# Routing weights of a tile computed beside its slot numbers instead of behind them

## The chip, the cores and the metric

The kernel runs on one core of a Trainium2 chip. The metric is the device time of one execution in microseconds (us), lower is better; the time of a kernel is the median of its runs. VectorE is DVE in the rows, ScalarE is ACT, TensorE is PE (its weight loads are PEld) and GpSimd is POOL.

## The reference, cut to what matters

The program is a block of four sublayers over 16 sequences of 112 tokens with 256 channels. The first is a transformer layer (self attention, cross attention to 375 context rows, gated feed-forward), the second a mixture of 64 experts with the best 8 for each token, the third a perceiver-like attention, the fourth a mixture of 8 experts with the best one. What the change touches is the router of the second sublayer:

```python
logits = jnp.einsum('bsh,he->bse', hidden_states, router_w)
affinity = jax.nn.sigmoid(logits)
top_scores, top_idx = jax.lax.top_k(affinity, K)                  # K = 8 of E = 64
top_w = top_scores / (jnp.sum(top_scores, axis=-1, keepdims=True) + 1e-09)
```

`top_w` is what the kernel calls `wgt`. It is used only in the third sublayer's stage, where the rows that the experts gave are added up (`add_rows`, L2034).

## The kernel before, in words

Each engine has a program of its own, and semaphores order them. Within an engine, instructions start in the order in which they are written. The first sublayer works on one sequence of 112 tokens ("batch" in the code) at a time: batch 0 is written out, batches 1 to 14 are a hardware loop, batch 15 is written out again. While batch b runs, the router works on the tile of batch b-1 (112 rows) in gaps that the code names by hand. The tile of batch 15 has no batch behind it: `tables0` does all its steps in a row.

The cross attention of a batch is the function `attention`. It has 16 heads, done as 8 pairs. Its loop has 9 steps on VectorE, s = 0 to 8. In step s PE writes the scores of pair s to PSUM (L759), VectorE takes their row maxima, two TENSOR_REDUCE to `nmax` (L1608), and ScalarE takes the exponentials (L1281). One step later PE transposes the probabilities (L774), VectorE and ScalarE copy one half each to `probsT` (L1612 and L1311), and one more step later PE multiplies them by the values (L786). ScalarE's order in a step is: exponential of the first head, copy of the pair before, exponential of the second head. PE's order in a step is: scores of pair s, transposes of pair s-1, outputs of pair s-2; the first three transposes wait for the two copies of the pair before and the first head's exponential, the next three for the second head's exponential.

At the end of step s VectorE calls `slots(r, 2s)` and `slots(r, 2s+1)` for the router's tile r. Calls 0 to 7 find the slot number of each of the 8 chosen experts, a SCALAR_TENSOR_TENSOR with an accumulator (L1697), call 0 also updates the counts (L1694), and call 8 casts the slot numbers to integers and releases them to GpSimd (L1701, `slots_ok`). GpSimd then copies them and issues 8 indirect DMAs that scatter the token numbers to a table in HBM (L536). Calls 8, 9, 10 and 12 also work out the weights: the sum of the 8 scores (L1703), plus 1e-9 (L1706), its reciprocal (L1709), and the product with the scores (L1712).

`settled()` waits until the last VectorE instruction that was issued through `note()` has finished writing, by a semaphore that VectorE raises itself; in the loop it takes a few register instructions to form the value waited for. Every slot call from 0 to 7 begins with one.

Behind the slot numbers of the last tile, `tables0` waits for the experts' counts, which PE forms once `slots_ok` is raised (L1004), and begins the block tables at L1810.

## Time and profile before

| what | value |
|---|---|
| median of 3 runs | 3499.01 us (3495.71 to 3500.59) |
| the profiled execution | 3510.26 us |
| its span, first to last instruction | 3508.5 us |
| mean granted TensorE clock | 0.926 of full speed |
| PE busy | 3049.2 us (87%) |
| DVE busy | 1495.2 us (43%) |
| ACT busy | 1078.9 us (31%) |
| POOL busy | 884.0 us (25%) |
| batches 1 to 15 in the trace | router step L1694 starts first at 179.5 us, then about every 98 us |

A row of a timeline has the start, the duration, the engine, the line, the operation, what it writes and reads, and how many instructions are merged in it; in square brackets stands how long the engine was idle before it, and what released it. "remote" there means that the profile shows no instruction whose end fits the release. A granted clock of 1.00 is TensorE at 2.4 GHz, 0.50 is 1.2 GHz.

### The profile page before, as it was taken

What the parts mean: (1) busy time and instruction counts of PE and PEld (TensorE: products, weight loads), DVE (VectorE), ACT (ScalarE), POOL (GpSimd) and SP (SyncE); (2) the same over time, 40 slices, a digit from 0 to 9 for tenths busy, and PEclk for the clock granted to TensorE, in tenths of its full rate; (3) what the DMA queues carried; (4) which work ended last, traced back from release to release, by engine and by line L of the source; (5) the groups of instructions that cost most, each with busy time, mean ns of one, the idle gap of its engine ahead of it and who ended that gap; (6) DMA issues with size and microseconds to landing.
All of it is one profiled execution on the core that took longest, in us unless ns stands there. A gap on an engine that the chain in (4) does not pass through costs nothing.

```text
span 3508.5 us, 59755 instructions
## 1 busy us (share of the span) xinstructions
PE 3049.2 (87%) x17314; PEld 2074.6 (59%) x17315; DVE 1495.2 (43%) x4297; ACT 1078.9 (31%) x2986; POOL 884.0 (25%) x1952
## 2 busy tenths in 40 slices
PE   6998989899898999885888885899999999995786
PEld 5666666666666666654666662555555555554564
DVE  3444444444444444444333332454544545434222
ACT  1333333333333333331222221343433434331111
POOL 0111111111111111112444443333242332401211
PEclk9999899999999999997999997899999999996898
DMA  5000000000000000003555541100000010002241
GB/s 191 5 3 6 4 6 6 6 6 6 6 1 6 4 6 6 6 2 102 162 171 172 152 104 37 30 15 30 15 24 21 15 30 15 15 1 84 99 149 56
DMA packets 89707, 155.44 MB, mean 44 GB/s; under 512 B 17072, under 2 KB 65072, under 8 KB 88112
## 3 DMA queue, kind: packets, MB, share of 16 engines
q1 hardware_dynamic: 39664, 85.56, 7.5%
q0 software_dynamic: 21184, 42.92, 4.8%
q10 hardware_dynamic: 28800, 26.23, 2.2%
q8 instruction: 32, 0.52, 0.1%
q14 instruction: 27, 0.22, 0.0%
HBM read 122.32 MB, written 32.32 MB: 44 GB/s over the span
## 4 chain that ended last, share of the span: by engine, by line
PE 74%; DVE 9%; issue 8%; ACT 3%; DMA 2%; another core or an unknown queue 2%; POOL 1%; DVEq 1%; POOLq 0%; SPq 0%; ACTq 0%
PE psG L812 12%; PE psG L806 11%; PE psG L800 11%; PE psG L822 7%; PE psG L1159 6%; PE psT L774 4%; PE psO L786 4%; PE psG L759 4%; DVE nmax L1608 3%; PE psO L1183 2%; PE psG L1165 2%; PE psO L1187 2%; ACT probs L1281 2%; PE psT L714 2%
## 5 line engine op out<-in xcount | busy, mean ns | idle before, releaser
L1281 ACT ACTIVATE probs<-psG,nmax 112x112 f32<-112x112 f32 (+2 forms) x768 | 403.8, 533 | 389.5 <-DVE nmax L1608 281.7
L812 PE MATMUL psG<-W,ctxT 128*125 128x512 f32 (+2 forms) x896 | 398.6, 593 | 0.0
L806 PE MATMUL psG<-ctxT,W 128*128 128x375 f32 (+1 forms) x1024 | 391.8, 530 | 1.1 <-ACT ctxT L1465 1.1
L800 PE MATMUL psG<-hT,W 128*128 128x112 f32 x2560 | 345.5, 293 | 45.9 <-issue 26.6
L1608 DVE TENSOR_REDUCE nmax<-psG 112x1 f32<-112x375 f32 (+1 forms) x512 | 287.2, 599 | 191.5 <-remote 106.1
L800 PEld LDWEIGHTS psG<-hT,W 128*128 128x128 f32 x2560 | 324.6, 206 | 71.8 <-issue 40.7
L774 PEld LDWEIGHTS psT<-ident,probs 112*125 112x125 f32 (+2 forms) x1792 | 215.5, 174 | 235.7 <-ACT probs L1281 133.6
L774 PE MATMUL psT<-ident,probs 112*125 112x112 f32 (+2 forms) x1792 | 275.4, 289 | 65.8 <-ACT probsT L1311 25.9
L806 PEld LDWEIGHTS psG<-ctxT,W 128*128 128x128 f32 x1024 | 189.8, 190 | 166.0 <-issue 114.6
L812 PEld LDWEIGHTS psG<-W,ctxT 128*125 128x125 f32 (+2 forms) x896 | 162.9, 186 | 187.7 <-issue 186.6
L759 PE MATMUL psG<-kT,qT 64*112 64x375 f32 (+1 forms) x1024 | 251.3, 568 | 11.5 <-ACT ctxT L1465 10.6
L786 PE MATMUL psO<-probsT,v 125*64 125x112 f32 (+2 forms) x3584 | 239.2, 274 | 0.5 <-issue 0.5
L597 POOL DMA_INDIRECT kT<-normed_rows,idc x200 | 194.4, 972 | 157.8 <-POOL idc L595 116.2
L1159 PE MATMUL psG<-W,kT 128*128 x704 | 215.7, 433 | 2.2 <-DVE kT L1982 0.6
L786 PEld LDWEIGHTS psO<-probsT,v 125*64 125x64 f32 (+2 forms) x3584 | 181.6, 141 | 30.8 <-DVE probsT L1612 2.6
L822 PE MATMUL psG<-W,oT 128*112 128x256 f32 x768 | 183.7, 394 | 0.1
L822 PEld LDWEIGHTS psG<-W,oT 128*112 128x112 f32 x768 | 141.3, 188 | 37.5 <-issue 8.2
L1281 ACT ACTIVATION_READ_ACCUMULATOR probs<-psG,nmax 112x1 f32 x768 | 157.0, 204 | 0.0
L1159 PEld LDWEIGHTS psG<-W,kT 128*128 128x128 f32 x704 | 131.8, 208 | 40.1 <-issue 26.0
L1612 DVE COPY probsT<-psT 125x336 f32<-125x336 f32 (+1 forms) x256 | 142.4, 556 | 28.8 <-PE psT L774 26.4
L1311 ACT ACTIVATE probsT<-psT 125x336 f32<-125x336 f32 (+1 forms) x256 | 125.2, 489 | 53.1 <-PE psT L774 31.9
L1431 ACT ACTIVATE mlp<-psG 128x128 f32<-128x128 f32 x176 | 48.8, 277 | 291.3 <-PE psG L1159 290.0
(318 smaller groups left out, 4089.7 us busy)
## 6 DMA issues: line engine op xcount, KB each, us to landing
expert_rows<-kT ACTq DMA_DIRECT2D x200, 128.0 KB
W<-in_ew SPq DMA_DIRECT2D x64, 384.0 KB
W<-in_ew SPq DMA_DIRECT2D x8, 2048.0 KB, 8.4
ctxT<-in_ctxT SPq DMA_DIRECT2D x16, 375.0 KB, 3.1
kT<-in_ctx SPq DMA_DIRECT2D x16, 375.0 KB
W<-in_eb SPq DMA_DIRECT2D x8, 640.0 KB, 9.5
kT<-normed_rows,idc POOLq DMA_INDIRECT x200, 3.0
W<-in_wq SPq DMA_DIRECT2D x2, 1024.0 KB, 9.2
```

The costliest lines, as they stand in the source:

```text
L597: nc.gpsimd.indirect_dma_start(out=xg[:, j.m, :], out_offset=None, in_=hd, in_offset=bass.IndirectOffsetOnAxis(ap=idc[:, j.m:j.m + 1], axi ...
L759: nc.tensor.matmul(psG[0:T, bank, 0:keys], qT[DH * i:DH * i + DH, s, :], kT[DH * i:DH * i + DH, s, 0:keys], start=True, stop=True).then_in ...
L774: mm = nc.tensor.transpose(psT[0:kn, i, c * T:(c + 1) * T], probs[:, 2 * (u % 2) + i, k0:k0 + kn], ident[0:T, 0:T])
L786: mm = nc.tensor.matmul(psO[DH * i:DH * i + DH, u // 4, (u % 4) * T:(u % 4 + 1) * T], v[0:kn, c, h * DH:(h + 1) * DH], probsT[0:kn, u % 2, ...
L800: mm = nc.tensor.matmul(bank[:, j * T:(j + 1) * T], wt[:, c, n0 + j * P:n0 + (j + 1) * P], hT[:, c, :], start=(c == 0), stop=(c == DC - 1))
L806: mm = nc.tensor.matmul(bank[:, 0:n], wt[:, c, n0 + j * P:n0 + (j + 1) * P], src[:, c, 0:n], start=(c == 0), stop=(c == DC - 1))
L812: mm = nc.tensor.matmul(bank[0:kn, 0:512], src[:, c, k0:k0 + kn], wt[:, c, n0 + half * 512:n0 + (half + 1) * 512], start=(c == 0), stop=(c ...
L822: mm = nc.tensor.matmul(bank[0:T, 0:D], oT_[:, c, :], wo[:, c, :], start=(c == 0), stop=(c == n - 1))
L1159: mm = nc.tensor.matmul(psG[:, 2 + j.m2, 0:256], xT[:, j.m2, c, :], W[:, bass.ds(base + 256 * c, 256)], start=(c == 0), stop=(c == DC - 1))
L1281: e = nc.scalar.activation(probs[:, slot, off:off + keys], psG[0:T, bank, off:off + keys], ACT.Exp, bias=nmax[:, h:h + 1], accum_out=rsum[ ...
L1608: nc.vector.tensor_reduce(nmax[:, 2 * s + i:2 * s + i + 1], psG[0:T, score_banks(s)[i], 0:keys], AXX, ALU.max, negate=True).then_inc(max_r ...
L1612: nc.vector.tensor_copy(probsT[0:size, (s - 1) % 2, 0, 0:nb * T], psT[0:size, 0, 0:nb * T]).then_inc(copied_dve, 1)
```

## The change

The four weight instructions move from calls 8, 9, 10 and 12 to calls 0, 1, 2 and 3, each directly behind that call's SCALAR_TENSOR_TENSOR. Calls 0 and 1 are at the end of attention step 0, calls 2 and 3 at the end of step 1. The slot numbers (L1701) stay in call 8, the end of step 4. The number of instructions and of `note()` calls per tile is the same. The three instructions that begin with `settled()` at the new place wait there for the slot instruction written just before them.

```diff
+            def weights(r, i):
+
+                if i == 0:
+                    note(nc.vector.tensor_reduce(wsum[:], topr[:], AXX, ALU.add))
+                if i == 1:
+                    settled()
+                    note(nc.vector.tensor_scalar(wsum[:], wsum[:], 1e-9, None, ALU.add))
+                if i == 2:
+                    settled()
+                    note(nc.vector.reciprocal(wsum[:], wsum[:]))
+                if i == 3:
+                    settled()
+                    nc.vector.tensor_scalar(wgt[:, bass.ds(r, 1), :].rearrange("t o k -> t (o k)"), topr[:], wsum[:],
+                                            None, ALU.mult)
+
             def slots(r, i):
...
                     note(nc.vector.scalar_tensor_tensor(repr_[:], iotaf[0:T, 0:64], tofr[:, i:i + 1], slotr[:],
                                                         ALU.is_equal, ALU.mult, accum_out=slofr[:, i:i + 1]))
+                    weights(r, i)
                 if i == 8:
                     settled()
                     nc.vector.tensor_copy(sloti[:, bass.ds(r, 1), :].rearrange("t o k -> t (o k)"),
                                           slofr[:]).then_inc(S0.slots_ok, 1)
-                    note(nc.vector.tensor_reduce(wsum[:], topr[:], AXX, ALU.add))
-                if i == 9:
-                    settled()
-                    note(nc.vector.tensor_scalar(wsum[:], wsum[:], 1e-9, None, ALU.add))
-                if i == 10:
-                    settled()
-                    note(nc.vector.reciprocal(wsum[:], wsum[:]))
-                if i == 12:
-                    settled()
-                    nc.vector.tensor_scalar(wgt[:, bass.ds(r, 1), :].rearrange("t o k -> t (o k)"), topr[:], wsum[:],
-                                            None, ALU.mult)
```

## Rows read from the trace of the kernel before

**Rows 1.** The page: busy time of the engines, and the chain by engine.

```profile
PE 3049.2 (87%) x17314; PEld 2074.6 (59%) x17315; DVE 1495.2 (43%) x4297; ACT 1078.9 (31%) x2986; POOL 884.0 (25%) x1952
...
PE 74%; DVE 9%; issue 8%; ACT 3%; DMA 2%; another core or an unknown queue 2%; POOL 1%; DVEq 1%; POOLq 0%; SPq 0%; ACTq 0%
```

**Rows 2.** The instructions that write wsum and wgt: count, min/median/max ns, first and last start.

```profile
L1703 DVE TENSOR_REDUCE wsum<-topr x16: 151/154/156, 188.6 to 1618.1; 112x1 f32<-112x8 f32 x16
L1706 DVE TENSOR_SCALAR wsum<-wsum x16: 153/153/154, 188.8 to 1618.3; 112x1 f32<-112x1 f32 x16
L1709 DVE RECIPROCAL wsum<-wsum x16: 151/152/164, 190.9 to 1618.6; 112x1 f32<-112x1 f32 x16
L1712 DVE TENSOR_SCALAR wgt<-topr,wsum x16: 219/221/288, 193.5 to 1618.8; 112x8 f32 x14, 112x8 f32<-112x8 f32 x2
```

**Rows 3.** The chain of waits in order of time, batch 2's attention: start, us, what.

```profile
276.28 0.14 DVE cumr L1694
...
277.20 0.47 DVE nmax L1608
...
278.83 1.06 PE psT L774 x6
```

**Rows 4.** The timeline of DVE, batch 2, attention steps 0 to 3.

```profile
276.91 0.28 DVE L1697 SCALAR_TENSOR_TENSOR repr<-iotaf,tofr,slotr 112x64 f32<-112x64 f32 x1
...
277.12 1.00 DVE L1608 TENSOR_REDUCE nmax<-psG 112x1 f32<-112x375 f32 x2
...
278.45 0.27 DVE L1697 SCALAR_TENSOR_TENSOR repr<-iotaf,tofr,slotr 112x64 f32<-112x64 f32 x1
...
279.05 1.00 DVE L1608 TENSOR_REDUCE nmax<-psG 112x1 f32<-112x375 f32 x2
...
281.47 1.00 DVE L1608 TENSOR_REDUCE nmax<-psG 112x1 f32<-112x375 f32 x2 [0.41 <-PE psG L759]
```

**Rows 5.** The timelines of PEld and ACT at step 3, batch 2.

```profile
281.36 0.73 PEld L774 LDWEIGHTS psT<-ident,probs 112*125 112x125 f32 x6 [0.54 <-ACT probs L1281]
...
280.97 0.21 ACT L1281 ACTIVATION_READ_ACCUMULATOR probs<-psG,nmax 112x1 f32 x1
```

**Rows 6.** The timelines of DVE and PE in `tables0`, the last tile.

```profile
1617.97 0.17 DVE L1701 CAST sloti<-slofr 112x8 int32<-112x8 f32 x1
1618.05 0.15 DVE L1703 TENSOR_REDUCE wsum<-topr 112x1 f32<-112x8 f32 x1
1618.32 0.15 DVE L1706 TENSOR_SCALAR wsum<-wsum 112x1 f32<-112x1 f32 x1
...
1618.84 0.23 DVE L1712 TENSOR_SCALAR wgt<-topr,wsum 112x8 f32<-112x8 f32 x1
1618.98 0.14 DVE L1810 TENSOR_SCALAR ecoli<-psG 64x1 int32<-64x1 f32 x1
...
1618.20 0.37 PE L1004 MATMUL psG<-ones,cumr 112*64 112x1 f32 x2 [4.17 <-DVE sloti L1701]
```

**Rows 7.** What L1608 waited for in all (us, times), and timelines of batches 2 and 15.

```profile
  remote: 106.1, 24
...
286.70 1.02 POOL L536 DMA_INDIRECT slot_table<-stt,st  x1 [0.80 <-POOL stt L533]
...
295.51 0.94 POOL L536 DMA_INDIRECT slot_table<-stt,st  x1 [0.30 <-issue]
...
290.43 0.22 DVE L1712 TENSOR_SCALAR wgt<-topr,wsum 112x8 f32 x1
298.25 1.00 DVE L1608 TENSOR_REDUCE nmax<-psG 112x1 f32<-112x375 f32 x2 [7.61 <-remote]
...
1560.22 0.91 PE L774 MATMUL psT<-ident,probs 112*125 112x112 f32 x6
...
1567.43 0.51 DVE L1612 COPY probsT<-psT 125x336 f32<-125x336 f32 x1 [1.60 <-remote]
```

**Rows 8.** Busy time of PE, PEld, DVE, ACT, POOL in a stretch of batch 2, then PEclk.

```profile
299.00:305.80 6.80, 5.98 (x34) 5.37 (x33) 2.03 (x5) 1.84 (x6) 0.00 (x0) 0.50 0.00 0
```

## The prediction

> **What bounds the kernel now.** I read the page first. PE is busy for 87% of the span and holds 74% of the chain, DVE 43% and 9% [rows 1]. So a VectorE edit matters only at the places where PE waits for VectorE. The instruction counts put the change there 16 times: 15 cross attentions (batches 1 to 15) and `tables0`; the four weight instructions are short, 0.15, 0.15, 0.15 and 0.22 us, 0.67 us a tile [rows 2]. Next I read the chain in order of time over one batch. It runs through PE nearly everywhere, but at the start of the cross attention it turns to VectorE: the counts, the slot instructions, then the row maxima of step 1, then the transposes on PE [rows 3]. So the work at the end of step 0 is on the path before the change. VectorE's timeline says how long that lasts. It runs without a gap from step 0 to step 2, its maxima 277.12 and 279.05, a period of 1.93 us, and is idle again, 0.41 us waiting for PE's scores, before 281.47 [rows 4]. From there the period is PE's, 2.42 us (279.05 to 281.47), and VectorE has room. The change takes work out of the part with room (steps 4 to 6) and puts it where there is none (steps 0 and 1).
>
> **What is added in steps 0 and 1.** The costs are distances from start to start, not durations, since two independent instructions overlap. Three distances serve:
> - An instruction that waits for nothing starts its duration less about 0.08 us after the one before: the reduce starts 0.08 behind the 0.17 us cast, L1810 0.14 behind L1712 [rows 6].
> - An instruction that waits by `settled()` for a small one starts 0.27 us behind it (1618.05 to 1618.32) [rows 6].
> - One that waits for a slot instruction starts 0.40 us behind it, as slot instructions do behind each other; the maxima, which don't wait for it, start 0.21 behind it (276.91 to 277.12) [rows 4].
>
> Step 0: slot, reduce, slot takes 0.21 + 0.27 = 0.48 in place of 0.40, so +0.08. Slot, add, maxima takes 0.40 + 0.07 = 0.47 in place of 0.21, so +0.26. The maxima of step 1 come 0.35 us later.
> Step 1: slot, reciprocal, slot takes 0.40 + 0.27 = 0.67; product and maxima take 0.40 + 0.14 = 0.54. Together 1.21 in place of 0.60 (278.45 to 279.05) [rows 4], so +0.61. The maxima of step 2 come 0.35 + 0.61 = 0.96 us later.
>
> **What of it reaches PE.** The first 0.35 reaches it whole: PE's transposes at 278.83 stand on the chain behind the maxima of step 1 by way of ScalarE's exponential and copy [rows 3]. For step 2 there is a little room. PE's next transposes start at 281.36 right behind its own scores; the second three of them need the exponential whose last part ends at 280.97 + 0.21 = 281.18 [rows 5]. A release takes about 0.06 (cast end 1618.14 to PE 1618.20) [rows 6], so they could start at 281.24. They start about half way through six weight loads of 0.73 us, near 281.69 [rows 5]. The room is 0.45 us. PE is late by the larger of 0.35 and 0.96 - 0.45 = 0.51: 0.51. In step 3 VectorE finds 0.41 us of idle time, so its maxima are late by 0.55 at 281.47, PE by 0.51, and the next exponential is within its room of 0.45 again. Nothing more is added; nothing is given back either, as PE has no idle time in steps 3 to 8 but the one below. 15 x 0.51 = 7.7 us.
>
> The bounds of a distance that no row shows at the new place: if each of the four costs only 0.08, as the cast and reduce do, VectorE is late by 0.32, less than the room, and PE by 0.16, or 2.4 us in all. If each costs a whole slot distance of 0.40, VectorE is late by 1.6, PE by 1.15, or 17 us. I take 7.7, since the same four instructions in the same dependencies are in rows 6.
>
> The Trainium skill, "Perfetto Trace Analysis", section Optimizing Scalar/DVE Operations, gives about 60 ns of engine time for a VectorE operation on SBUF. By that alone four operations would be 0.24 us and PE would be late by 0.12, in all 1.8 us. The rows have 0.15 us and more for one, and 0.27 with the wait, and the measurement decides here.
>
> **What is removed.** Steps 4 to 6 lose 0.67 us of instructions. VectorE waits for PE's scores there, so this gives nothing. No DMA is moved, but what `slots_ok` starts is: the cast stays in step 4, and steps 3 and 4 are late by PE's 0.51, so GpSimd's 8 scatters come 0.51 us later, at the same place relative to PE. They end long before the next tile's.
>
> **`tables0`.** All is in a row there. Added ahead of the cast: 0.08 + (0.40 + 0.25 - 0.40) + 0.27 + 0.14 = 0.74. Removed behind it: L1810 came 1.01 us behind the cast; it needs PE's counts, which end at 1618.20 + 0.37 = 1618.57, 0.60 behind the cast, so with the release it can come 0.66 behind it [rows 6]. That gives back 0.35. Net +0.4 us, between -0.3 and +0.9. The scatters of this tile start 0.74 later, and the stage behind them doesn't begin with them.
>
> **Sum.** 7.7 + 0.4 = 8.1 us on the profiled 3510.3, which is 3518.4. The median of the runs is 11 us below the profiled execution; the same steps are in both, so 3499.0 + 8.1 = 3507. My own range for this case is 3502 to 3513.
>
> **Rivals.**
> *It is hidden.* If the four distances are near the low bound or PE has more room than I read, PE loses 0.16 to 0.4 us a batch, and the time is 3501 to 3505. For it: VectorE is only 43% busy. Against: the chain passes through these very instructions [rows 3], and no idle time stands between them.
>
> *A stall goes away, and the kernel is much faster.* In each of the 15 batches VectorE stands still before the maxima of step 7, right behind L1712: 7.61 us in batch 2 [rows 7], 106 us of "remote" idle time in all. GpSimd issues its 8 scatters at that time, from 286.70 to 295.51, and L1712 at 290.43 is in their midst. After the change no weight instruction is there. If L1712 were what blocks VectorE, up to 7.2 us of a stall would go, less 2 us in which PE does work that it has to do anyway. The half-clock stretch behind the stall, 6.80 us at 0.50 [rows 8], could go as well, worth 3.4 us. That is 5.2 to 8.6 us a batch, 78 to 129 in all, less 8: 3378 to 3429, say 3404. It decides from the point where any instruction that L1712 holds up is the one that VectorE stands on. Against it: what VectorE waits for is a PE semaphore, and PE's are late for others too. In batch 15 the transposes stand at 1560.22 and are over at 1561.13, but the copy whose only wait is theirs starts at 1567.43, after 1.60 us in which VectorE had nothing in hand [rows 7]. So signals of PE come late while the scatters run, whatever VectorE does, and the change moves neither.
> The Trainium skill, "SBUF — State Buffer", section Who interferes with whom, has this rival's mechanism: a VectorE tensor_scalar in a 2-port mode and a GpSimd instruction lock each other out of a shared port pair. L1712 is such an instruction, from SBUF to SBUF. By this rule the time would be that of this rival; by the rows it is 3507, as GpSimd's scatters run on through the stall, the last at 295.51 with its usual 0.30 us before it [rows 7].
>
> *The clock.* PE's idle time at the start of the attention grows by 0.51 us. If that adds half-clock stretches, each of 6.8 us costs 3.4 us [rows 8]. In 5 to 15 batches that is 17 to 51 us more, 3524 to 3558. For it: half-clock stretches follow PE's stalls. Against: 0.5 us is small beside the 7 us stall before the one in rows 8.
>
> **How the numbers follow.** The forecast has 0.62, hidden 0.20, the stall that goes 0.08, the clock 0.10. A change of 0.2%, 7 us here, is about what a measurement can tell from none. The forecast is just past it at 8.1, and I give six tenths of it to beyond: slower 0.62 x 0.6 + 0.10 = 0.47; same 0.62 x 0.4 + 0.18 = 0.43; faster 0.08 + 0.02 = 0.10. The range leaves out the stall rival and most of the clock rival, and takes in the bounds of 2.4 and 17 us and the spread of the runs: 3497 to 3520.
>
> **What would show it.** In the trace after: the maxima of step 1 start 0.47 us behind the second slot instruction in place of 0.21, and 2.54 us lie between the maxima of steps 1 and 2 in place of 1.93; the idle time before step 3's maxima gone or below 0.1; PE's transposes of step 3 waiting 0.1 to 0.2 us for an exponential; the wait before step 7 still 6 to 8 us and still "remote"; L1810 0.66 us behind the cast. I am wrong if the step 7 wait is gone, if the batch is not 0.3 to 0.7 us longer at full clock, or if the granted clock moves by more than 0.005.

## The result, and the profile after

The changed kernel takes 3529.1 us (median of 4 runs, 3525.8 to 3533.0), the kernel before 3499.6 us (4 runs): a ratio of 1.0079, 95% interval 1.0062 to 1.0096. It is slower by 29.5 us; the forecast was 8.1, and the range ended at 3520.

The page after, of which the first two lines are the page's head and busy times, and the third its chain by engine:

```profile
span 3527.5 us, 59755 instructions
...
PE 3060.5 (87%) x17314; PEld 2081.8 (59%) x17315; DVE 1499.2 (43%) x4297; ACT 1082.5 (31%) x2986; POOL 887.5 (25%) x1952
...
PE 73%; DVE 9%; issue 8%; ACT 3%; another core or an unknown queue 3%; DMA 2%; POOL 1%; DVEq 1%; POOLq 0%; SPq 0%; ACTq 0%
```

No busy time on it has moved by more than 1% [rows 1]. PE is busy 11.3 us longer with the same 17314 matmuls, and the mean granted clock fell from 0.926 to 0.921: a first sign that the clock has a part in it.

VectorE's timeline over attention steps 0 to 3, one batch (start, us, engine, line, operation, and in brackets the idle time before it); the batch's counts (the router instruction that opens a tile, L1694 before) start at 570.6:

```profile
570.95 0.28 DVE L1712 SCALAR_TENSOR_TENSOR repr<-iotaf,tofr,slotr 112x64 f32<-112x64 f32 x1
...
571.16 0.15 DVE L1693 TENSOR_REDUCE wsum<-topr 112x1 f32<-112x8 f32 x1
571.42 0.28 DVE L1712 SCALAR_TENSOR_TENSOR repr<-iotaf,tofr,slotr 112x64 f32<-112x64 f32 x1
...
571.82 0.15 DVE L1696 TENSOR_SCALAR wsum<-wsum 112x1 f32<-112x1 f32 x1
571.93 1.00 DVE L1608 TENSOR_REDUCE nmax<-psG 112x1 f32<-112x375 f32 x2
...
573.92 0.29 DVE L1712 SCALAR_TENSOR_TENSOR repr<-iotaf,tofr,slotr 112x64 f32<-112x64 f32 x1
...
574.41 0.23 DVE L1702 TENSOR_SCALAR wgt<-topr,wsum 112x8 f32 x1 [0.20 <-DVE repr L1712]
574.54 1.00 DVE L1608 TENSOR_REDUCE nmax<-psG 112x1 f32<-112x375 f32 x2
...
576.47 1.00 DVE L1608 TENSOR_REDUCE nmax<-psG 112x1 f32<-112x375 f32 x2
```

The maxima of step 1 start 0.51 us behind the second slot instruction (571.42 to 571.93; before 0.21) and those of step 2 2.61 us later (before 1.93); the idle time before step 3's is gone [rows 4]. So far it is what was forecast, a little larger.

What wasn't forecast is seen on PE. Here are its timelines over the same steps of this batch and of the next:

```profile
572.07 0.89 PE L759 MATMUL psG<-kT,qT 64*112 64x375 f32 x4
573.64 1.06 PE L774 MATMUL psT<-ident,probs 112*125 112x112 f32 x6 [0.68 <-ACT probsT L1311]
574.63 0.80 PE L786 MATMUL psO<-probsT,v 125*64 125x112 f32 x12
575.36 0.89 PE L759 MATMUL psG<-kT,qT 64*112 64x375 f32 x4
...
577.97 0.89 PE L759 MATMUL psG<-kT,qT 64*112 64x375 f32 x4
```

```profile
670.30 0.89 PE L759 MATMUL psG<-kT,qT 64*112 64x375 f32 x4
671.87 1.57 PE L774 MATMUL psT<-ident,probs 112*125 112x112 f32 x6 [0.69 <-ACT probsT L1311]
673.37 1.39 PE L786 MATMUL psO<-probsT,v 125*64 125x112 f32 x12
674.69 1.59 PE L759 MATMUL psG<-kT,qT 64*112 64x375 f32 x4
...
678.94 0.89 PE L759 MATMUL psG<-kT,qT 64*112 64x375 f32 x4
```

From the scores of step 2 to those of step 4 it is 577.97 - 572.07 = 5.90 us in the one batch and 8.64 us in the other, and the same 12 output matmuls take 0.80 and 1.39 us. The windows name the cause (length, then busy time of PE, PEld, DVE, ACT and POOL, then PEclk):

```profile
573.60:580.40 6.80, 6.75 (x64) 4.68 (x64) 5.82 (x22) 4.52 (x16) 0.00 (x0) 1.00 0.00 0
671.90:678.70 6.80, 6.80 (x38) 5.06 (x40) 4.39 (x18) 3.47 (x12) 0.00 (x0) 0.50 0.00 0
```

A stretch at half the clock (1.2 GHz in place of 2.4), 38 matmuls where the other has 64, lies in steps 2 to 4, right behind the pause that the weight instructions have lengthened. Reading all clock records of both traces: after, such a stretch of 6.8 us begins some 3 us behind the counts in every second batch (those with counts at 471, 669, 867, 1065, 1263 and 1461; one of 3.4 us at 375), and makes the scores of step 4 2.75 us late each time; before there was one, of 3.4 us, at 377. The batches between them have the same two pauses and no stretch, so the pause alone doesn't say which batch is hit. From 180 to 1560 us the kernel before spends 198 us at half clock and the changed one 232.

Last, what VectorE's maxima waited for (us in total, times):

```profile
  PE psG L759: 97.8, 119
  remote: 75.4, 21
```

The wait at step 7 is still there and still "remote", but shorter: 5.1 us in 13 of the 15 batches and never more, where before it was 6.1 to 7.8 us in 13 of them [rows 7]. No weight instruction is near it now.

PE's hand-over at this place is shorter too. Before, the transposes of step 7 start 1.57 us behind its scores (1.5 to 3.0 in 13 of the 14 loop batches), after 0.82 (in all 14). These are PE's rows of a batch before with its counts at 1156.6, and of the batch after with its counts at 570.6:

```profile
1170.51 0.89 PE L759 MATMUL psG<-kT,qT 64*112 64x375 f32 x4
1172.08 1.06 PE L774 MATMUL psT<-ident,probs 112*125 112x112 f32 x6 [0.68 <-issue]
```

```profile
585.11 0.89 PE L759 MATMUL psG<-kT,qT 64*112 64x375 f32 x4
585.93 0.98 PE L774 MATMUL psT<-ident,probs 112*125 112x112 f32 x6
```

Both batches have their half-clock stretches at the same places, near 23 and 74 us behind the counts, and they take 98.42 and 98.23 us: where no new stretch comes in, the lateness of steps 1 and 2 is gone by the end of the batch.

### The profile page after: what moved, and what is told of

The parts are those of the page before. It is cut to its first block, busy times and chain, and to the rows that moved or that the text cites. A ratio compares the mean times of both kernels' runs of the same rounds, so it can differ in the third digit from the quotient of the medians.

```text
span 3527.5 us, 59755 instructions
## 1 busy us (share of the span) xinstructions
PE 3060.5 (87%) x17314; PEld 2081.8 (59%) x17315; DVE 1499.2 (43%) x4297; ACT 1082.5 (31%) x2986; POOL 887.5 (25%) x1952
## 4 chain that ended last, share of the span: by engine, by line
PE 73%; DVE 9%; issue 8%; ACT 3%; another core or an unknown queue 3%; DMA 2%; POOL 1%; DVEq 1%; POOLq 0%; SPq 0%; ACTq 0%
PE psG L812 12%; PE psG L806 11%; PE psG L800 10%; PE psG L822 7%; PE psG L1159 6%; PE psT L774 4%; PE psO L786 4%; PE psG L759 4%; DVE nmax L1608 3%; PE psO L1183 2%; PE psG L1165 2%; PE psO L1187 2%; ACT probs L1281 2%; PE psT L714 2%
## 5 line engine op out<-in xcount | busy, mean ns | idle before, releaser
L1608 DVE TENSOR_REDUCE nmax<-psG 112x1 f32<-112x375 f32 (+1 forms) x512 | 286.4, 600 | 176.9 <-PE psG L759 97.8
L774 PE MATMUL psT<-ident,probs 112*125 112x112 f32 (+2 forms) x1792 | 282.6, 295 | 69.0 <-ACT probsT L1311 39.0
L759 PE MATMUL psG<-kT,qT 64*112 64x375 f32 (+1 forms) x1024 | 255.5, 576 | 11.5 <-ACT ctxT L1465 10.6
L1999 DVE TENSOR_TENSOR mlp<-mlp,psG 128x128 f32<-128x128 f32 x176 | 50.7, 288 | 205.5 <-ACT mlp L1431 203.2
```

What stands on the lines that cost most here:

```text
L759: nc.tensor.matmul(psG[0:T, bank, 0:keys], qT[DH * i:DH * i + DH, s, :], kT[DH * i:DH * i + DH, s, 0:keys], start=True, stop=True).then_in ...
L774: mm = nc.tensor.transpose(psT[0:kn, i, c * T:(c + 1) * T], probs[:, 2 * (u % 2) + i, k0:k0 + kn], ident[0:T, 0:T])
L1608: nc.vector.tensor_reduce(nmax[:, 2 * s + i:2 * s + i + 1], psG[0:T, score_banks(s)[i], 0:keys], AXX, ALU.max, negate=True).then_inc(max_r ...
```

## The experiments

Eighteen experiments on four chips. Since the chips differ more than the kernels, I call the chip of the comparison above A, and the others B, C, D and E (A may be one of C to E). Each kernel ran beside the kernel before on its chip. "Loop" is the time from the counts of the first tile to those of the last, 15 batches, in the profiled execution; what follows the loop took 1893 to 1901 us in all of them, with no order in it, so the loop is the more precise measure of a change in it. The ratio is that of the comparison, and not quite that of the medians where runs fall apart. All kernels of mine have one register operation more than the two given ones, ahead of a wait of TensorE in the expert stage:

```
-                        pe.wait_ge(s.loaded, rank + 1)
+                        pe.reg_alu(loaded_reg, pe.to_reg(rank + 1), 1, ALU.max)
+                        pe.wait_ge(s.loaded, pe.snap(loaded_reg))
```

| chip | kernel | median us (runs) | ratio to before | loop us |
|---|---|---|---|---|
| A | before | 3499.6 (4) | | 1435.0 |
| A | after | 3529.1 (4) | 1.0079 | 1451.3 |
| B | before, with the register operation | 3397.8 (11) | 1.0004 | 1319.1 |
| B | after | 3407.8 (9); 3405.9 (6) | 1.0038; 1.0029 | 1328.6; 1331.6 |
| B | weights at both places | 3424.5 (5) | 1.0086 | 1345.9 |
| B | no weights | 3398.4 (11) | 1.0004 | 1318.5 |
| B | weights behind the mask | 3396.4 (11) | 1.0002 | 1320.7 |
| B | after + transposes | 3407.3 (6) | 1.0035 | 1328.7 |
| B | both places + transposes | 3412.5 (5) | 1.0049 | 1335.4 |
| C | before + 5 us at step 7 | 3515.9 (12) | 1.0043 | 1434.2 |
| C | after + 5 us at step 7 | 3529.2 (5) | 1.0080 | 1452.3 |
| C | the same + transposes | 3534.2 (5) | 1.0095 | 1452.8 |
| C | weights ahead of the slots | 3527.9 (11) | 1.0053 | 1416.7 |
| D | after | 3534.5 (5) | 1.0045 | 1454.7 |
| D | after + transposes | 3524.3 (11) | 1.0017 | 1449.3 |
| D | weights behind the mask | 3499.3 (5) | 0.9947 | 1427.5 |
| D | before, scatters late | 3426.3 (5) | 0.9741 | 1352.2 |
| E | before, scatters late | 3428.4 (5) | 0.9747 | 1351.7 |
| E | after, scatters late | 3431.0 (5) | 0.9757 | 1359.6 |

The kernel before itself took 3396 us on B, 3501 on C (3492 to 3522), 3518 on D (3510 to 3521) and 3515 on E.

**The base, on chip B.** The edit is the register operation alone.

> The kernel before, with one register instruction more in PE's expert loops (a lower bound of 1 on a value that is waited for). All experiments have it, so this is their base. Expected: 3500 us, within 5; the block of the first sublayer as before: first router step at about 179 us, last at 1614 us, the scores of step 7 waited for 6.7 to 8.2 us.

3397.8 us, 1.0004 (0.9995 to 1.0012): the operation costs no time there, and so the kernels can be compared. It does raise the mean granted clock, 0.944 to 0.947 against 0.941 to 0.943 of the kernel before beside it, so clocks are compared below between kernels that all have it, where that can be done. No run has it alone on C, D or E. The expected 3500 us fell: the kernel before runs 103 us faster than on A, and its trace says where. The "remote" wait doesn't exist; PE's scores are the only thing that the maxima of all steps waited for:

```profile
L1611 DVE TENSOR_REDUCE nmax<-psG x512: 534/590/667, 89.4 to 3057.6; 112x1 f32<-112x375 f32 x86, 112x1 f32<-112x487 f32 x85
its engine sat idle before it (us, times) until:
  PE psG L759: 91.0, 142
```

> The changed kernel on that same base. Expected: 29 us above e0_before, within 5. In every second batch a half-clock stretch of 6.8 us in attention steps 3 and 4; step 7 waits 5.2 us.

3407.8 us, 10.0 over the base where 29 was expected. The scores of step 4 start 7.34 us behind the counts in place of 6.73 in every loop batch: 0.61 late, 15 x 0.61 = 9.2, and the loop is 9.5 us longer. No stretch at half clock in steps 2 to 4, with 116 us of it from 180 to 1560 against 123. So the direct term stands alone in this execution. One of the nine runs took 3431.6 us at a clock of 0.936, where the others have 3402 to 3412 at 0.944 to 0.948; it has no trace, but its clock is that of a kernel with the stretches.

**Both places, and none.** The first has the late four instructions beside the early ones, the second has neither and sets `wgt` to 0.125 once.

```
+                    note(nc.vector.tensor_reduce(wsum[:], topr[:], AXX, ALU.add))   # i == 8, and 9, 10, 12 as before
```

```
-                    note(nc.vector.tensor_reduce(wsum[:], topr[:], AXX, ALU.add))   # and 9, 10, 12
+            nc.vector.memset(wgt[:], 0.125)
```

> The four weight instructions stand at both places: in steps 0 and 1, and again in steps 4 to 6. Theory 'early' (all the loss comes from what VectorE does more in steps 0 and 1, directly and by the half-clock stretch that it calls): as e0_after, 25 to 32 us above e0_before, with the stretch in steps 3 and 4 of every second batch, and step 7 waits 5.2 us as in e0_after. Rival 'removal' (taking L1709 and L1712 out of steps 5 and 6, where GpSimd scatters, shortens the wait of step 7 from 8.1 to 5.2 us and so shifts all that follows): step 7 waits 8.1 us again, and the time is 10 us or more above e0_after, as the shorter wait is not earned.

> The weights of the experts are not worked out at all (wgt is set to 0.125 once); nothing else is changed. Theory 'early': the later place costs and gives nothing, so as e0_before within 4 us, step 7 waits 8.1 us, no stretch in steps 3 and 4. Rival 'removal': step 7 waits 5.2 us, 2 to 3 us less in each of 15 batches, 3455 to 3470 us.

Without weights 3398.4 us, as the base: taking the late instructions away gives nothing here, so what the change costs on this chip is what it adds. This says nothing of a chip with the wait at step 7, which this one hasn't. With both places 3424.5, 26.7 over the base where 10 was expected of the early place alone. The early lateness is 0.61 again, but here the stretches of A appear on chip B: seven batches have one in steps 2 to 4 (455.5, 1005.1 and 1281.6 of 6.8 us, 363.4, 820.8, 912.9 and 1189.4 of 3.4 us), and the granted clock is 0.940 against 0.946. So the stretches aren't a matter of the chip alone. Why the late instructions beside the early ones bring them is open.

**Another place.** The four instructions behind the selection mask, ahead of the attention:

```
                     nc.vector.tensor_scalar(mskr[:], repr_[:], -1.0, None, ALU.is_equal).then_inc(S0.mask_ok, 1)
+                    chain(nc.vector.tensor_reduce(wsum[:], topr[:], AXX, ALU.add))
+                    chain(nc.vector.tensor_scalar(wsum[:], wsum[:], 1e-9, None, ALU.add))
+                    chain(nc.vector.reciprocal(wsum[:], wsum[:]))
+                    nc.vector.tensor_scalar(wgt[:, bass.ds(r, 1), :]..., topr[:], wsum[:], None, ALU.mult)
```

> The four weight operations stand behind the selection mask (L1683), in a row, where VectorE has 2.6 us without work while TensorE computes the gate projection (L800); nothing of them stands in the attention any more, early or late. Theory A (what counts is the place: an instruction of VectorE between two maxima of attention steps 0 to 3 delays the tile, one in a wait doesn't): same time as the kernel before, within 0.1%, scores of step 4 at +6.73 us behind the counts as before. Rival B (any work added to VectorE's thread ahead of the attention delays the tile by its own length, about 0.8 us x 15): 10 to 12 us over the kernel before.

1.0002 (0.9993 to 1.0011). VectorE's timeline shows why it is free:

```profile
269.07 0.15 DVE L1687 TENSOR_REDUCE wsum<-topr 112x1 f32<-112x8 f32 x1
...
269.33 0.15 DVE L1688 TENSOR_SCALAR wsum<-wsum 112x1 f32<-112x1 f32 x1
...
269.59 0.16 DVE L1689 RECIPROCAL wsum<-wsum 112x1 f32<-112x1 f32 x1
...
269.95 0.23 DVE L1690 TENSOR_SCALAR wgt<-topr,wsum 112x8 f32 x1 [0.20 <-DVE wsum L1689]
...
271.75 0.62 DVE L1628 TENSOR_SCALAR qT<-psG 128x448 f32<-128x448 f32 x1 [1.57 <-PE psG L800]
```

The four take 1.11 us and are followed by 1.57 us in which VectorE waits for PE anyway. (These rows are of the same kernel's run on chip D.) So on chip B it is the place that costs, not the work.

**Does TensorE's pause call the stretches?** Six more transposes in each of steps 0 and 1, into the bank that the real ones overwrite:

```
+                        if u < 2:
+                            for _ in range(extra):          # 6
+                                nc.tensor.transpose(psT[0:T, 0, 0:T], ident[0:T, 0:T], ident[0:T, 0:T])
                         for i in range(2):
                             pe.wait_ge(probs_ready, u0 + 2 * u + i + 1)
```

> The changed kernel, with six more transposes of the identity on TensorE ahead of the transposes of attention steps 0 and 1 of each batch (into the bank that these overwrite at once). They stand in TensorE's wait for the probabilities (1.17 and 1.16 us between two matmuls, 0.79 us in the second of them before the change) and keep it at work there; VectorE's instructions are those of the changed kernel. Theory A (the longer pause of TensorE at the attention's second step is what calls the additional half-clock stretches of 6.8 us in steps 3 and 4): no half-clock stretch in those steps in any batch, the tile's 0.61 us stays, so 10 us over the kernel before on whatever chip. Rival B (the stretches hang on the batch's period or the chip, not on that pause): as many stretches as the changed kernel has beside it on the same chip, and its time, plus nothing or more if the six transposes come late to the probabilities (0.1 us a step, 3 us in all).

> The changed kernel once more, beside the others. Theory A (two parts: 0.61 us a tile, 10 us in all, everywhere; and extra half-clock stretches in attention steps 3 and 4, of some 2.8 us a batch where they come, that depend on the place and the run): 10 us over the kernel before and no such stretches, or about 30 us over with 6 or more of them, the difference between the two cases being 2.8 us times their number. Rival B (the change costs one fixed amount on a given chip, whatever the half-clock stretches): a time that doesn't follow their number.

> The kernel that works the weights out at both places (27 us over the kernel before, with half-clock stretches in attention steps 3 and 4 of seven batches), with six more transposes of the identity on TensorE ahead of the transposes of attention steps 0 and 1. Theory A (TensorE's pause calls the stretches): the stretches go, and it comes to 10 us over the kernel before. Rival B (the later place itself, four instructions between maxima of steps 8 to 12, costs the 17 us): it stays at 25 us over or more.

On chip B the changed kernel had one such stretch (at 181.1), and took 3405.9 us; with the transposes it has none and takes 3407.3. That tells little. The kernel with both places tells more: its stretches in steps 2 to 4 fall from seven to none, and its time from 28.1 to 16.6 us over the kernel before (ratios 1.0086 and 1.0049, intervals apart). Theory A asked for 10: 0.69 x 15 = 10.4 are the lateness in steps 1 and 2, where the transposes themselves add 0.08, and 6 us remain, 0.4 a batch, behind step 7. I have no cause for these.

**Is it the wait at step 7?** Sixteen sums on VectorE stood for A's wait of 5 to 8 us:

```
+                if i == 13:
+                    for k in range(16):
+                        nc.vector.tensor_reduce(idled[:, k:k + 1], norms[:, 0, :], AXX, ALU.add)
```

> The kernel before, with sixteen sums over 256 columns on VectorE (some 5 us, into columns that nothing reads) ahead of the maxima of attention step 7 of each batch: they stand for the wait of 5 to 8 us that both kernels showed there on the first chip and that this chip doesn't have. Both theories: 5 us x 15 and the time to come back into step, so some 75 to 110 us over the kernel before; half-clock stretches behind that wait (on the first chip one began at +20 to +23 us in nearly every batch). It is the base for the next two.

> The changed kernel with the same sixteen sums ahead of the maxima of step 7. Theory A (on the first chip the wait at step 7 made the difference between +10 and +29 us, since TensorE's pauses at the attention's start and at step 7 together call further half-clock stretches): 20 us or more over the kernel before with the same sums, with half-clock stretches of 6.8 us in attention steps 3 and 4 of several batches. Rival B (what differs between the chips is not that wait): 9 to 12 us over it, no more stretches than it has.

> As the kernel ahead of this one in the list, with the six transposes of the identity on TensorE ahead of the transposes of attention steps 0 and 1. Theory A: no half-clock stretch in steps 3 and 4 in any batch, and 10 us over the kernel before with the sums. Rival B: the same time as without the transposes, within 3 us.

These three ran on chip C, which has the wait itself, so the sums mostly ran inside it and the base rose by 15 us and not by 75. As an imitation it fails. It shows one thing: with a pause of 8 us there in both kernels the change costs 13 us in the medians and 18 in the loop, and neither kernel has a stretch in steps 2 to 4; half-clock time behind step 7 grows instead, from 12.4 to 15.6 us a batch. The transposes take 5 us more and give nothing. Theory A had 20 us or more and stretches in steps 3 and 4, rival B 9 to 12 us; the size lies between them, and the stretches of theory A aren't there.

**A cheaper order at the same place.** Each weight instruction ahead of the slot instruction of its call, so that one wait serves both:

```
                 if i < 8:
                     settled()
+                    weights(r, i)          # without a settled() of its own
                     note(nc.vector.scalar_tensor_tensor(repr_[:], iotaf[0:T, 0:64], ...))
-                    weights(r, i)
```

> The changed kernel with each weight instruction written ahead of the slot instruction of its call, so that one wait on the step count serves both. By the start-to-start distances (0.27 us between two maxima where a slot instruction already stands, and 0.40 us with a wait of its own) each costs 0.13 us less: steps 0 to 3 come 0.61 - 2 x 0.13 = 0.35 us late a tile, 5 us in all over the kernel before. If the wait ahead of an instruction costs nothing (rival): 10 us over it, as the changed kernel.

VectorE's timeline, steps 0 and 1:

```profile
464.83 0.16 DVE L1696 TENSOR_REDUCE wsum<-topr 112x1 f32<-112x8 f32 x1
464.91 0.27 DVE L1713 SCALAR_TENSOR_TENSOR repr<-iotaf,tofr,slotr 112x64 f32<-112x64 f32 x1
...
465.30 0.15 DVE L1698 TENSOR_SCALAR wsum<-wsum 112x1 f32<-112x1 f32 x1
465.37 0.27 DVE L1713 SCALAR_TENSOR_TENSOR repr<-iotaf,tofr,slotr 112x64 f32<-112x64 f32 x1
...
465.57 0.99 DVE L1611 TENSOR_REDUCE nmax<-psG 112x1 f32<-112x375 f32 x2
```

3527.9 us in the median, 27 us over the kernel before beside it, where 5 were expected (or 10, by the rival). In step 0 the two weight instructions add 0.08 and 0.06 us here (0.46 between the slot instructions in place of 0.40), where the changed kernel adds 0.07 and 0.30: what is dear is the wait of its own, not the instruction. The scores of step 4 are 0.14 us late a tile, less than the 0.35 that I had expected. And yet the runs on chip C fall apart: 3494, 3499, 3504, 3509 and 3513 us at a clock of 0.935 to 0.929, and six at 3528 to 3531 us at 0.923 to 0.925. One and the same kernel has executions up to 36 us apart, and the mean granted clock falls as their time grows. In the profiled run (3494, to which the loop time in the table belongs) no stretch lies in steps 2 to 4; none of the longer ones has a trace. What decides between them is open.

**The second kind of chip once more.** On chip D:

> The changed kernel once more, wanted on a chip of the first kind (kernel before at 3500 us, TensorE's signals late at step 7). Theory A (0.61 us a tile of direct lateness, which a chip of that kind partly gives back in the wait at step 7, and a batch rhythm that falls on more half-clock time there): 3525 to 3533 us in every run, at a mean granted clock of 0.921 to 0.922, against 3492 to 3522 us at 0.921 to 0.931 for the kernel before; on the other kind of chip 10 us over the kernel before. Rival B (the four runs of the first comparison were chance, since the kernel written with the weights ahead of the slots ran at 3494 to 3531 us there): runs spread over 3500 to 3533 us.

> The changed kernel with six transposes of the identity ahead of the transposes of attention steps 0 and 1. On the other kind of chip (first measured) they took nothing and gave nothing. On a chip of the first kind, theory A (TensorE's pause there calls the stretches of steps 3 and 4): none of them in those steps, and 10 to 20 us less than the changed kernel beside it. Rival B (the half-clock time only moves, to behind the wait at step 7): no stretch in steps 3 and 4 either, but the time of the changed kernel within 5 us, as the pair with the sixteen sums showed (3529 and 3534 us).

> The weights behind the mask, none in the attention. On the other kind of chip it ran as the kernel before (ratio 1.0002). Theory A (what the chip of the first kind adds follows from the lateness of steps 1 and 2): as the kernel before here too, within 5 us. Rival B (any shift of VectorE's instructions changes the rhythm): 10 us or more off it, either way.

The changed kernel took 3528 to 3535 us in all five runs, the one with nothing in the attention 3496 to 3503: 35 us apart in the medians, 29 between the profiled executions and 27 in the loop, though they differ in the place of four instructions. This pair is the cleanest account of what the early place costs.

But the kernel with nothing in the attention is also 18 us below the kernel before (0.9934 to 0.9961), where its expectation had no more than 5: theory A fell there, and rival B, 10 us or more off, came in. So on D the change is a gain of 18 us and a loss of 35. The gain would go with the four late instructions of steps 4 to 6 that both kernels lack; that isn't shown, as neither the kernel before nor the register operation alone has a trace on D.

The mean batch of each (14 periods, from the same records as the scores' times) in three parts:

| us | counts to scores of step 7 | from there to the second maximum of step 7 | rest of the batch | period |
|---|---|---|---|---|
| weights behind the mask | 13.87 | 7.43 | 75.74 | 97.04 |
| after | 15.65 | 7.49 | 75.61 | 98.76 |
| after + transposes | 14.56 | 7.46 | 76.52 | 98.54 |

All of the difference between the first two is ahead of step 7: 1.78 us, of which 0.61 is the direct lateness, and 6 stretches of 2.75 us over 14 batches are 1.18. With the transposes every stretch in steps 2 to 4 is gone, in all batches; one of the windows, at the same place as above:

```profile
575.20:582.00 6.80, 6.80 (x70) 4.96 (x70) 5.89 (x22) 4.44 (x16) 0.00 (x0) 1.00 0.00 0
```

against the changed kernel on the same chip:

```profile
575.40:582.20 6.80, 6.80 (x40) 5.02 (x40) 4.28 (x18) 3.45 (x12) 0.00 (x0) 0.51 0.00 0
```

Seen on PE's timeline, the transposes (L773) close the first of the two pauses and stand behind the second:

```profile
570.32 1.52 PE L759 MATMUL psG<-kT,qT 64*112 64x375 f32 x8
571.77 0.79 PE L773 MATMUL psT<-ident 112*112 112x112 f32 x6
572.54 1.14 PE L777 MATMUL psT<-ident,probs 112*125 112x112 f32 x6
573.61 0.89 PE L759 MATMUL psG<-kT,qT 64*112 64x375 f32 x4
575.10 0.79 PE L773 MATMUL psT<-ident 112*112 112x112 f32 x6 [0.61 <-ACT probsT L1318]
```

So the stretches hang on how much work TensorE has there; that is shown by two pairs, on chips B and D. Which of the two pauses counts isn't: the change lengthens the second, and the transposes close the first. They give back 10 us in the medians (3534.5 to 3524.3) and 5 in the loop, not the whole 17 of the stretches: 0.91 us a batch are lost again behind step 7. Theory A (10 to 20 us less) just holds by the medians, and rival B (the time moves to behind step 7) has a good part of it.

**The wait at step 7 itself.** GpSimd's scatters moved behind the sum R2b of the same batch, in the kernel before:

```
-                if not first:
-                    scatter_tile(b - 1)
                 wait_apart(pool, dve_evac, JOBS_BEFORE + DVE_JOBS * b + R2_JOB - 2 * last)
...
                 if not first:
+                    scatter_tile(b - 1)
                     wait_apart(pool, S0.scat_a, 16 * L0E.K * b)
```

> The kernel before, with the tile's scatters on GpSimd (eight indirect DMAs, 286.7 to 295.5 us in batch 2) issued behind the sum R2b instead of ahead of it, so some 20 us later in the batch, beside the MLP. Theory A (TensorE's late signals, 7 us in the wait for step 7's scores on a chip of the first kind, come while the scatters are issued, and cost most where VectorE and TensorE hand each other work every microsecond): the wait at step 7 goes there, the attention's second half starts 7 us earlier, and the time falls by 50 us or more of the 15 x 7; GpSimd's R2b, ready earlier, adds nothing. Rival B (it follows the batch, not the scatters): the wait stays at step 7. On a chip without the late signals: no change, within 3 us, by either.

3426.3 us against 3517.5 on the same chip, 0.9741 (0.9728 to 0.9754): 91 us less, for two lines moved. In the batch with its counts at 546.1 GpSimd now issues them from 579.80 on:

```profile
578.01 0.73 POOL L549 TENSOR_TENSOR R2b<-R2b,X 112x256 f32<-112x256 f32 x1 [0.25 <-POOL R2b L548]
...
579.80 1.02 POOL L536 DMA_INDIRECT slot_table<-stt,st  x1 [0.81 <-POOL stt L533]
...
588.60 0.94 POOL L536 DMA_INDIRECT slot_table<-stt,st  x1 [0.30 <-issue]
```

Step 7's maxima start 0.92 us behind their scores (559.95 to 560.87), with the product of the weights (L1714 here) still right ahead of them; without scatters beside it, it holds nothing up:

```profile
559.82 0.22 DVE L1714 TENSOR_SCALAR wgt<-topr,wsum 112x8 f32 x1
560.87 1.00 DVE L1610 TENSOR_REDUCE nmax<-psG 112x1 f32<-112x375 f32 x2 [0.82 <-PE psG L758]
```

and the late signal has gone where the scatters went, into the MLP:

```profile
591.48 1.06 DVE L1772 SCALAR_TENSOR_TENSOR mlp<-psG,cols,mlp 128x112 f32<-128x112 f32 x4 [8.25 <-remote]
```

There it costs less. How much is an estimate: what follows step 7's second maximum takes 76.3 us a batch here and 74.0 us on chip B, which has no late signals, so some 2 us a batch. That TensorE's long products there cover the rest is likely and not shown. With the wait the half-clock stretch behind it goes too: one stretch is left in nearly every batch, and the granted clock is 0.944 to 0.945, against 0.924 to 0.927 of the changed kernel on the same chip.

> The kernel before with the scatters behind the sum R2b, as base for the next one on the same chip. On a chip of the first kind: 3426 us as measured, no wait at step 7, one half-clock stretch a batch instead of two. On the other kind, where the kernel before takes 3396 us and has no wait at step 7: within 5 us of it.

> The changed kernel with the scatters behind R2b. Theory A (what the change costs is 0.61 us a tile wherever the wait at step 7 and the half-clock stretch that follows it are absent, and the 10 to 20 us more on a chip of the first kind come through these two): scores of step 4 0.61 us late in every batch, 9 to 11 us over the kernel of the last line on the same chip, whichever kind it is, and a clock within 0.002 of it. Rival B (the change itself brings the half-clock stretches on a chip of the first kind, scatters or not): 20 us or more over it there, with stretches of 6.8 us in steps 3 and 4 of half the batches.

On E the two differ by 2.7 us in the medians, 3425 to 3431 against 3429 to 3434, which the intervals of their ratios don't tell apart, and by 7.8 us in the loop. Steps 0 to 6 are 0.61 us late in the 11 batches without a stretch there; 3 have one. Some 0.5 us of a batch is regained between 67 and 77 us behind the counts, where the one remaining half-clock stretch now begins 0.9 us earlier in the batch. Rival B, 20 us or more, has fallen. Theory A's 9 to 11 holds for the loop nearly and for the whole kernel not: part is given back, and the three stretches weren't in it. So the change costs 3 to 8 us here, and 13 to 30 (C, D and A) where the wait at step 7 is left in.

## Why the prediction was wrong

**The distances.** Forecast 0.21, 0.27 and 0.40 for a start behind an independent, a small and a slot instruction. Measured 0.21, 0.26 and 0.40; the product stands 0.49 behind its slot instruction where 0.40 was forecast, and the maxima 0.11 and 0.13 behind the weight instruction ahead of them. The sums: step 1's maxima 0.38 us late (0.35 forecast), step 2's 1.07 more behind the scores than before, which were not late themselves (0.96 forecast).

**The room of PE.** 0.61 us late a batch in place of 0.51: the scores of step 4 start 7.34 us behind the counts in place of 6.73. With `tables0` (its cast 3.50 and 4.24 us behind the counts, 0.74 late as forecast, and the next instruction 0.64 behind it, forecast 0.66) that is 15 x 0.61 + 0.4 = 9.6 us where 8.1 stood. Chip B gives 10.0, twice. The mechanism was right on that chip and this term off by a fifth.

**"Nothing more is added; nothing is given back either", and the sum 3499.0 + 8.1.** This is the step that failed. It took the batch at the clock that it had. On A, with TensorE's second pause 0.37 us longer, a half-clock stretch came into steps 2 to 4 of every second batch: six of them at 2.75 us are 16.5 us, and a shorter one was there before and after. "Nothing is given back" failed too: in batches without a new stretch the 0.61 us are regained at step 7 (98.42 us before, 98.23 after). The mean of the 14 batches in three parts: ahead of step 7 +1.76 us (0.61 direct, the rest stretches), from there to the second maximum of step 7 -2.35, in the rest +1.78; together +1.19, or 16 of the 19 us between the two profiled executions. I have no cause for the last two parts, which nearly cancel. The other 10.6 of the 29.5 us lie between the profiled execution of before, 3510.3, and its other runs; the prediction took "the same steps are in both" for granted, and no trace shows one of the shorter runs.

**"What is removed": nothing.** On B that held (no weights at all: as the base). On D the kernel with nothing in the attention is 18 us below the kernel before, and on A the wait at step 7 fell from 6.8 to 4.9 us in the mean once the late instructions were gone. So on the chips with the wait this term may have been a gain that the stretches hid. Against it, on C the kernel before with the sums has the late four and yet the short hand-over of 0.82 us at step 7 in every loop batch. No pair of traces on one such chip, with and without the late four alone, settles it.

**The rival "the clock".** It had the right mechanism (TensorE's longer pause, stretches of 6.8 us, in 5 to 15 batches) and the right time, 3524 to 3558, and a chance of 0.10. The argument against it was that 0.5 us is small beside the 7 us stall that precedes the stretch of rows 8. That compared it with the wrong neighbour. The pauses of steps 0 and 1 were 1.17 and 0.79 us before and 1.17 and 1.16 after, counted from the start of one matmul to the start of the next, and one batch of the kernel before already had the stretch, at 377 us, with the same two pauses as its other batches. That was the row to ask for: a warning that the kernel was near it. That the time fell into the rival's 3524 to 3558 is in part luck, as 10.6 us of it are the profiled execution's distance from the other runs. The criterion named there, a clock that moves by more than 0.005, was set too wide: 0.005 x 3527 is 17.6 us of TensorE's work already.

**The rival "a stall goes away".** It fell as it stood: the wait stays, "remote", without a weight instruction near, and the time rose. In part it had something: the wait is 2 us shorter (4.9 in place of 6.8 in the mean), though nothing was gained on the whole. The kernel without any weights doesn't test it, as it ran on the chip without the wait. That the scatters make TensorE's signals late was argued from batch 15 [rows 7]; moving them has shown it. The lock between a VectorE tensor_scalar and GpSimd that the Trainium skill, "SBUF — State Buffer", section Who interferes with whom, describes is not what makes this wait, since it stays at 5.1 us on A and at up to 7.3 us on D with the tensor_scalar elsewhere. Whether the lock adds the 2 us on A, no run shows.

**"Hidden"** fell with the 0.61 on chip B. The sign of the forecast, slower, was right, on A for another reason than the one forecast; with that batch read, the range had to reach the clock's 3524 to 3558.

**What stays open.** Why chips A, C, D and E show the late signals and B not; which batches get a stretch; where the 18 us on D come from; why step 7's maxima, which start 7.50 us behind their scores in the mean batch of A before, start 5.05 behind them after, when on D it is 6.16 with the weights in the attention and 5.80 without; and why executions of one kernel on one chip are up to 36 us apart.

## What to carry to other kernels

Ask of an added wait not only how late it makes the engine that sets the end, but whether the clock already falls behind that place somewhere in the trace; one such batch in the trace before is a warning that many may follow. Small work beside a tight hand-over is cheap if it shares a wait that is there already (0.06 to 0.08 us in step 0) and dear with a wait of its own (0.30 us there), and free in front of a wait for PE (on chip B). And look past the change: the largest loss found here, 91 us a run, was a wait called "remote" that stood beside GpSimd's scatters, and it went when these were issued beside long products.

## What the runs showed of the hardware

- The same kernel takes 3396 us on one chip and 3500 to 3518 us on others. Of the two traces of it, B's loop is 116 us shorter, and only A's has signals of TensorE that come late while GpSimd issues indirect DMAs. They hold VectorE for 5 to 8 us once a batch on A, C and D (on E 8 us, seen in the MLP), never on B.
- The late signals go with the scatters, from attention step 7 to the MLP, and the kernel is 91 us shorter with them there. On B moving them wasn't tried.
- Half-clock stretches stand at three places of a batch: 17 to 27 us behind the counts, which goes with the wait at step 7; 3 us behind them, in some batches, which goes away with twelve small transposes a batch; and 65 to 78 us behind them in nearly every batch on every chip, which nothing here took away.
- The mean granted clock sorts the runs of one kernel (weights ahead of the slots, chip C): 0.935 and 0.934 at 3494 and 3499 us, 0.932 and 0.929 at 3504 to 3513, 0.923 to 0.925 at 3528 to 3531.
- Best of all that ran on D and E: the kernel before with the scatters late, 3426 and 3428 us. It is 91 and 86 us below the kernel before there, and on D 108 below the changed one; with the changed weights and late scatters it is 3431 on E.
